# A Fourier gate whose norms and inner products are taken from the features in space

## The chip, the cores and the metric

The kernel runs on one core of one Trainium2 chip. The metric is the device time of one execution in microseconds; the median of 3 executions of the kernel before is 333.0 us (332.04 to 333.19). The core has these engines: PE (TensorE, matrix products; PEld is its weight load), DVE (VectorE), ACT (ScalarE, activation functions), POOL (GpSimd) and SP (which starts transfers). Each engine works through its own list of instructions in order and waits on semaphores for the others.

## The reference, cut to what matters

The program is a chain of seven layers in float32 on an input of 8 images, 32 channels, 16 x 16 points: group norm and deformable convolution, the Fourier gate, an attention with landmarks and a pseudo-inverse, a mixture of experts, four layers of linear attention, and a routed layer whose operations depend on the data. The change lies in the Fourier gate alone:

```
feat = gelu(batchnorm(conv2d(x, conv_w, padding=3, dilation=3)))     # 8 images, 16 channels
F2   = fft2(feat)                                                   # complex
qkv  = F2.reshape(B, 8, 2, N)                                       # heads of two channels; q = k = v
q    = qkv / sqrt(sum(re**2 + im**2, over N) + 1e-6)
attn = einsum('bhdn,bhen->bhde', q, conj(q)) * tau                  # 2 x 2 for each head, complex
attn = softmax(attn.real) + 1j * softmax(attn.imag)
out_f = abs(ifft2(attn @ qkv))
cg   = sigmoid(cg2_w * gelu(bn(conv1x1(F2.real, cg1_w))) + cg2_b)
gate = abs(ifft2(cg * F2))
y    = concatenate([out_f, gate]) + x
```

N is 256 points. For real a and b and their transforms A and B, the sum over N of A conj(B) is N times the sum over N of a b, which is real; so the norm of A is taken from a, and the imaginary part of the inner product is zero.

## The kernel before, in words

The 8 images x 16 channels of `feat` fill the 128 partitions, and the 256 points are the columns (tile `feat`, 128 x 256). The kernel is written by hand: each engine has one function (`_(pe)`, `_(act)`, `_(dve)` and so on), its order is the order of the text, and the semaphores tie them. `link` on DVE makes the next instruction wait for the end of this one. `then_inc(S["..."])` raises a semaphore, `wait_ge` waits for it. Small values of a partition stand in the columns of the tile `small`.

The gate goes as follows, and all of it stands between the convolution (L614) and the first layer norm of the tokens (L1329 by way of `centre`, L1476):

- ACT makes `feat` by a Gelu (L1119). PE transposes it (L621), ACT copies the transposed tile (L1121), and PE multiplies with a table of sines and cosines into `F2`, real and imaginary part side by side, 128 x 512 (L628). ACT copies that to SBUF (L1123).
- PE makes two products with a matrix that swaps the two channels of a head: of `feat` (L625, bank 5) and of `F2` (L633, bank 4). A float32 matmul shows in the trace as two instructions ("passes") or more; a transpose as one.
- The branch of the gate: PE L632, then on ACT a Gelu (L1126) and a Sigmoid (L1127) make `cg`; DVE multiplies `F2` by it (L1449, two halves, semaphore `gated`); PE transposes the result (L646), ACT copies it (L1131), PE transforms it back (L651), ACT squares (L1137), DVE adds real and imaginary squares (L1473), ACT takes the root (L1139, semaphore `abs` at 2).
- The branch of the attention: DVE takes sums of squares and products of `F2` and its swapped copy `mixed` (L1437 to L1445, a custom instruction that reads out a sum, so two records each), adds the 1e-6 (L1452, `l2_sum`), ACT takes roots (L1129), DVE works out the four scores of each head (L1454 to L1461, `sm2_in`), ACT takes their exponentials (L1133), DVE makes the weights and mixes `feat` and the swapped `feat` in space (L1463 to L1471), ACT takes the root (L1135, `abs` at 1).
- PE gathers both into the tokens (L659, first from `outf`, then from `gatef`), and its last product lets DVE go on with the layer norm (L1329). Between these steps PE runs `keep_busy(n)`: n products of 512 columns, two passes each, whose results nobody reads (L528). In this stretch there are `keep_busy(4)` ahead of the wait for `gated`, `keep_busy(4)` behind L651, and `keep_busy(7)` behind L659.

On ACT an `ACT_TABLE_LOAD` is put in by the compiler where a function needs another table than the one before it; the text of the kernel doesn't name it, and the trace gives it the line of the activation that it serves. The layers behind the gate wait for its output by semaphores, each in turn; the weights for them are all loaded before the gate begins (`late_in`), but for the records of the routed layer, whose transfers are started by SP when PE, at the end of the landmark attention, raises `oT_mm`, or by the steps of the routed layer themselves.

Of the kernel before, what the change touches and what calls it, by code (L numbers as in the profile page):

```python
# [20 lines left out]
ACT = mybir.ActivationFunctionType  # L21
# [3 lines left out]
N = HH * WW  # L25
# [79 lines left out]
FFT_EV = {"featT": 1, "f2": 2, "gT": 3}  # L105


class Own:
# [5 lines left out]
    def link(self, ins):  # L114
        self.n += 1
        ins.then_inc(self.sem, 1)
        self.eng.wait_ge(self.sem, self.n)
# [7 lines left out]
def build(nc, x, cst, w32, par, rows, toep, w_out, moe_w1, moe_w2, moe_b2, am, fm, codes, rec_a, rec_b, out):  # L125
    ctx = ExitStack()
    with ctx:
# [3 lines left out]
        S = {n: ctx.enter_context(nc.semaphore(n)) for n in SEMS}  # L131
        ps = [ctx.enter_context(nc.psum_tensor(f"ps{i}", [P, 512], F32))[:, :] for i in range(8)]
# [13 lines left out]
        def cst_(n):  # L146
            return cstb[:, CST[n][0]:CST[n][1]]
# [31 lines left out]
        small = sb("small", 512)  # L179
# [16 lines left out]
        feat = sb("feat", N)  # L196
        featT = sb("featT", PT * P).rearrange("p (t n) -> p t n", t=PT)
        F2 = ar(18432, 2 * N)
        mixed = ar(18944, 2 * N)
# [321 lines left out]
        def _(pe):  # L521
# [3 lines left out]
            def keep_busy(count, lhs=None, rhs=None, bank=7, cols=512):  # L525

                for _ in range(count):
                    mm(ps[bank][:, 0:cols], ident if lhs is None else lhs, (xC if rhs is None else rhs)[:, 0:cols],  # L528
                       start=True, stop=True)
# [103 lines left out]
            mm(ps[4], cst_("swap"), F2, start=True, stop=True).then_inc(S["swap_mm"], 1)  # L633
# [8 lines left out]
            keep_busy(4)  # L642
# [11 lines left out]
            keep_busy(4)  # L654
# [418 lines left out]
        def _(act):  # L1073
# [47 lines left out]
            af(featT.rearrange("p t n -> p (t n)"), ps[2][:, 0:PT * P], ACT.Copy).then_inc(S["fft_ev"], 1)  # L1121
            act.wait_ge(S["fft_mm"], FFT_MM["f2"])
# [5 lines left out]
            act.wait_ge(S["l2_sum"], 1)  # L1128
            af(small[:, 18:20], small[:, 16:18], ACT.Sqrt).then_inc(S["l2_std"], 1)  # L1129
            act.wait_ge(S["fft_mm"], FFT_MM["gT"])  # L1130
            af(gT.rearrange("p a t n -> p (a t n)"), ps[7], ACT.Copy).then_inc(S["fft_ev"], 1)  # L1131
            act.wait_ge(S["sm2_in"], 1)
            af(small[:, 28:32], small[:, 28:32], ACT.Exp).then_inc(S["sm2_exp"], 1)  # L1133
# [183 lines left out]
        def _(dve):  # L1317
# [110 lines left out]
            for reach in (1, 2, 4, 8, 16, 32):  # L1428
# [5 lines left out]
            Fp, fp = ps[4], ps[5][:, 0:N]  # L1434
            dve.wait_ge(S["fft_ev"], FFT_EV["f2"])
            sm = small
            link(v_.tensor_tensor_reduce(scr, F2, F2, 1.0, 0.0, ALU.mult, ALU.add, sm[:, 16:17]))  # L1437
            dve.wait_ge(S["swap_mm"], 2)
            link(v_.tensor_copy(mixed, Fp))
            link(v_.tensor_tensor_reduce(scr, mixed, mixed, 1.0, 0.0, ALU.mult, ALU.add, sm[:, 17:18]))  # L1440
            link(v_.tensor_copy(sm[:, 20:21], sm[:, 16:17]))
            link(v_.tensor_tensor_reduce(scr, F2, mixed, 1.0, 0.0, ALU.mult, ALU.add, sm[:, 21:22]))
            link(v_.tensor_tensor_reduce(scr[:, 0:N], F2[:, N:2 * N], mixed[:, 0:N], 1.0, 0.0, ALU.mult, ALU.add,
                                         sm[:, 22:23]))
            link(v_.tensor_tensor_reduce(scr[:, 0:N], F2[:, 0:N], mixed[:, N:2 * N], 1.0, 0.0, ALU.mult, ALU.add,  # L1445
                                         sm[:, 23:24]))
            dve.wait_ge(S["cg_act"], 1)
            for a in range(2):
                tt_(gated[:, a * N:a * N + N], F2[:, a * N:a * N + N], cg, ALU.mult).then_inc(S["gated"], 1)  # L1449
            link(tt_(sm[:, 23:24], sm[:, 22:23], sm[:, 23:24], ALU.subtract))  # L1450
            link(v_.memset(sm[:, 22:23], 0.0))
            ts_(sm[:, 16:18], sm[:, 16:18], 1e-6, None, ALU.add).then_inc(S["l2_sum"], 1)  # L1452
            dve.wait_ge(S["l2_std"], 1)
# [7 lines left out]
            tt_(ex, pairs, sm[:, 20:22].unsqueeze(2).to_broadcast([P, 2, 2]), ALU.subtract).then_inc(S["sm2_in"], 1)  # L1461
            dve.wait_ge(S["sm2_exp"], 1)
# [426 lines left out]
```

## Time and profile before

| | |
|---|---|
| median of 3 executions | 333.0 us (332.04 to 333.19) |
| the profiled execution's own time | 331.74 us |
| its span, first to last instruction | 330.0 us |
| granted TensorE clock, mean | 0.982 of full speed |
| busy: PE, PEld, DVE, ACT, POOL | 294.5, 199.4, 189.0, 154.4, 35.1 us |
| the Fourier gate, `feat` to the layer norm | 89.91 to 110.03 us |

Times in the rows are microseconds from the span's start. An engine's busy time counts its filling products too: PE's 89% is in part `keep_busy`. In a row, the share in brackets at the end is the idle time of the engine before it and what released it. Ends of matmuls are modelled, and neighbouring ones overlap in the record; the distance from start to start is the safer measure.

### The profile page before, as it was taken

Reading aid. Unit: us, or ns where it says so; the run is one execution under the profiler, and the core shown is the slowest. Engines: PE = TensorE matmul, PEld = TensorE weight load, DVE = VectorE, ACT = ScalarE, POOL = GpSimd, SP = SyncE. Lnnn points to the kernel's source line nnn. Section 1 sums busy time; section 2 is a strip of 40 time slices with the busy share of each in tenths; the row PEclk is TensorE's granted clock in tenths of the full one; section 3 lists DMA queues with packets and bytes.
Section 4 is the critical chain, followed back from the end, with each engine's and each line's share of the span. In section 5 each row is a group of like instructions: output and inputs, shape, how many; then the busy total and the mean of one; then the engine's idle time right before and its main releaser. Section 6 shows DMA issues by size and latency. Waiting matters only on the chain.

```text
span 330.0 us, 6721 instructions
## 1 busy us (share of the span) xinstructions
PE 294.5 (89%) x2064; PEld 199.4 (60%) x2064; DVE 189.0 (57%) x452; ACT 154.4 (47%) x336; POOL 35.1 (11%) x34
## 2 busy tenths in 40 slices
PE   7999999999999989999999989989996779777980
PEld 3665677777444437898999645668952266226620
DVE  4594998883346676478887564462261156225720
ACT  2097766667154256445566033112203448644840
POOL 5300062000100014000220000024200000000010
PEclk9999999999999999999999999999998799999997
DMA  2954300000000000000000033333100100000000
GB/s 84 248 113 89 88 9 2 2 0 2 2 0 0 0 1 2 0 2 0 3 0 0 0 58 62 68 68 63 31 2 3 21 2 0 19 19 0 0 18 32
DMA packets 9386, 9.17 MB, mean 28 GB/s; under 512 B 4080, under 2 KB 8944, under 8 KB 9072
## 3 DMA queue, kind: packets, MB, share of 16 engines
q1 hardware_dynamic: 9096, 8.53, 11.7%
q8 instruction: 15, 0.25, 0.3%
q10 hardware_dynamic: 264, 0.30, 0.3%
q14 instruction: 11, 0.08, 0.1%
HBM read 8.57 MB, written 0.26 MB: 27 GB/s over the span
## 4 chain that ended last, share of the span: by engine, by line
PE 32%; DVE 10%; issue 4%; ACT 2%; DMA 2%; DVEq 2%; SPq 0%; POOL 0%; ACTq 0%; POOLq 0%
PE ps L759 3%; PE ps L765 3%; DMA recA<-rec_a 2%; PE ps L915 2%; PE ps L999 2%; PE ps L1055 2%; PE ps L1002 2%; PE ps L528 2%; PE ps L1047 2%; PE ps L905 1%; PE ps L897 1%; PE ps L1012 1%; PE ps L776 1%; PE ps L806 1%; DVE arena L1562 1%
## 5 line engine op out<-in xcount | busy, mean ns | idle before, releaser
L528 PE MATMUL ps<-xC,cstb 128*128 128x512 f32 (+3 forms) x134 | 57.3, 554 | 0.0
L1407 DVE TENSOR_TENSOR arena<-arena 128x512 f32 x72 | 44.3, 684 | 7.8 <-ACT arena L1107 4.6
L1114 ACT ACTIVATE arena<-ps 128x512 f32<-128x512 f32 x72 | 37.7, 603 | 15.7 <-PE ps L585 15.6
L528 PEld LDWEIGHTS ps<-xC,cstb 128*128 128x128 f32 x134 | 23.7, 192 | 24.1 <-issue 23.9
L585 PE MATMUL ps<-cstb,arena 128*128 128x128 f32 x288 | 36.3, 277 | 0.7 <-DVE arena L1407 0.7
L585 PEld LDWEIGHTS ps<-cstb,arena 128*128 128x128 f32 x288 | 31.0, 140 | 9.4 <-DVE arena L1407 8.6
L593 PE MATMUL ps<-arena 128*32 128x256 f32 x288 | 19.2, 385 | 0.0
L1275 ACT ACTIVATE arena<-ps,rmax 128x256 f32<-128x256 f32 x32 | 14.7, 479 | 2.6 <-DVE rmax L1738 2.4
L759 PE MATMUL ps<-arena 128*128 128x160 f32 x96 | 14.5, 304 | 0.3 <-DVE arena L1590 0.3
L1055 PE MATMUL ps<-arena,w2c 128*32 128x512 f32 x32 | 12.0, 719 | 1.9 <-ACT arena L1306 1.9
L497 POOL TENSOR_TENSOR arena<-w32b,cstb 128x1024 f32<-128x1024 f32 x4 | 7.6, 1893 | 57.5 <-PEq L891 45.8
L759 PEld LDWEIGHTS ps<-arena 128*128 128x128 f32 x96 | 13.3, 190 | 0.5 <-DVE arena L1590 0.4
L1306 ACT ACTIVATE arena<-ps,w2c 128x512 f32<-128x512 f32 x16 | 9.7, 688 | 7.6 <-PE ps L1047 7.6
L999 PE MATMUL ps<-cstb 128*128 128x256 f32 x28 | 9.3, 414 | 3.3 <-ACT arena L1275 3.3
L1082 ACT ACTIVATE small<-small 128x16 f32<-128x16 f32 x5 | 1.1, 216 | 23.3 <-DVE small L1333 22.4
L1738 DVE TENSOR_REDUCE rmax<-ps 128x2 f32<-128x512 f32 x16 | 10.3, 683 | 2.8 <-PE ps L990 2.5
L765 PE MATMUL ps<-arena,bdY 128*128 128x64 f32 x96 | 11.5, 273 | 0.3 <-DVE arena L1581 0.3
L765 PEld LDWEIGHTS ps<-arena,bdY 128*128 128x128 f32 x96 | 11.2, 192 | 0.5 <-DVE arena L1581 0.5
L593 PEld LDWEIGHTS ps<-arena 128*32 128x32 f32 x288 | 7.5, 109 | 6.3 <-ACT arena L1114 3.1
L453 POOL TENSOR_SCALAR cgw<-cstb,parb 128x128 f32<-128x128 f32 x1 | 7.1, 7096 | 33.3 <-DMA codeB<-codes 33.3
L506 POOL TENSOR_TENSOR ln_a<-tC,hC 128x512 f32<-128x512 f32 x1 | 1.3, 1268 | 84.6 <-DVE hC L1792 84.6
L1002 PE MATMUL ps<-cstb,arena 128*128 128x128 f32 x64 | 9.3, 273 | 0.0
(373 smaller groups left out, 529.0 us busy)
## 6 DMA issues: line engine op xcount, KB each, us to landing
arena<-rec_a SPq DMA_DIRECT2D x19, 128.5 KB
toepb<-toep SPq DMA_DIRECT2D x1, 1536.0 KB
w32b<-w SPq DMA_DIRECT2D x1, 1225.0 KB
cstb<-cst SPq DMA_DIRECT2D x1, 1044.0 KB
recA<-rec_a SPq DMA_DIRECT2D x4, 128.5 KB
arena<-rec_b SPq DMA_DIRECT2D x19, 16.5 KB
w1b<-moe_w SPq DMA_DIRECT2D x1, 264.0 KB
xC<-x SPq DMA_DIRECT2D x1, 256.0 KB, 2.6
```

The costliest lines, as they stand in the source:

```text
L528: mm(ps[bank][:, 0:cols], ident if lhs is None else lhs, (xC if rhs is None else rhs)[:, 0:cols], start=True, stop=True)
L585: last = tr(ps[c % BI][:, (q * PT + t) * P:(q * PT + t + 1) * P], ST[:, c, t, q * 8:q * 8 + 8, :], ident)
L593: last = mm(ps[4 + g][32 * bi:32 * bi + 32, 0:N], GS[:, g, q, bi, k, :], SQ[:, g * BI + bi, q, :], start=False, stop=last_one and q == PT - 1,
L759: last = mm(ps[q][:, 160 * j:160 * j + 160], bdY[:, b, :], YV[:, b, :], start=True, stop=True)
L765: last = mm(ps[q][:, 320 + 64 * j:384 + 64 * j], bdY2[:, 2 * q + j, :, :], pG[:, 2 * q:2 * q + 2, :], start=True, stop=True)
L999: mm(ps[a][:, 0:N], ident, cstb[:, 0:N], start=True, stop=True)
L1002: last = tr(ps[a][:, (u * PT + t) * P:(u * PT + t + 1) * P], pr[:, a * 512 + t * N + u * P:a * 512 + t * N + u * P + P], ident)
L1055: last = mm(ps[1][32 * bi:32 * bi + 32, :], w2c[:, 0:C], f1[:, 512 * bi:512 * bi + 512], start=True, stop=True)
L1114: af(SQ[:, c].rearrange("p q n -> p (q n)"), ps[c % BI], ACT.Copy).then_inc(S["s_ev"], 1)
L1275: last = af(pr[:, b * 512 + t * N:b * 512 + t * N + N], ps[b][:, t * N:t * N + N], ACT.Exp, bias=rmax[:, 2 * b + t:2 * b + t + 1], accum_o ...
L1407: tt_(ST[:, c], hy.unsqueeze(3).to_broadcast([P, PT, 16, 16]), hx.unsqueeze(2).to_broadcast([P, PT, 16, 16]), ALU.mult).then_inc(S["prod"], 1)
L1738: v_.tensor_reduce(rmax[:, 2 * b:2 * b + 2], arr3(ps[b], N), AX.X, ALU.max, negate=True).then_inc(S["sc_max"], 1)
```

## The change

PE's product of the swap matrix with `F2` (two passes) is gone, and both `keep_busy(4)` around the inverse transform become `keep_busy(2)`. On DVE the sums are taken over `feat` and over its swapped copy (256 columns instead of 512), scaled by N; this begins when `feat` is there instead of `F2`; the two sums of the imaginary part are gone, and their columns are set to zero. The scores are worked out ahead of the wait for `cg_act`, and the two multiplications by `cg` stand behind them. On ACT the root of the norms stands ahead of the copy of `F2`, between the Gelu of `feat` and the Gelu of `cg`; the exponential of the scores stands behind the Sigmoid and ahead of the copy of `gT`.

```diff
--- before.py
+++ after.py
@@ -630,7 +630,6 @@
             pe.wait_ge(S["fft_ev"], FFT_EV["f2"])
             pe.wait_ge(S["pool_bd"], 5)
             mm(ps[6][:, 0:N], cgw, F2[:, 0:N], start=True, stop=True).then_inc(S["fft_mm"], 1)
-            mm(ps[4], cst_("swap"), F2, start=True, stop=True).then_inc(S["swap_mm"], 1)
 
             pe.wait_ge(S["x1_ready"], 2 * BG)
             mm(ps[1], zeros, cstb[:, 0:512], start=True, stop=False, skip_group_check=True)
@@ -639,7 +638,7 @@
                     mm(ps[1][:, (t * BG + g) * P:(t * BG + g + 1) * P],
                        x1C[:, g * N + t * P:g * N + t * P + P], ident, start=False, stop=False,
                        skip_group_check=True)
-            keep_busy(4)
+            keep_busy(2)
             pe.wait_ge(S["gated"], 2)
             for a in range(2):
                 for t in range(PT):
@@ -651,7 +650,7 @@
                 last = mm(ps[2], gT[:, a, t, :], dft[:, t, a * N:a * N + 2 * N], start=(n == 0), stop=(n == 3))
             last.then_inc(S["fft_mm"], 1)
 
-            keep_busy(4)
+            keep_busy(2)
             T1 = ps[1].rearrange("p (t b c) -> p t b c", t=PT, b=B)
             for n, src in enumerate((outf, gatef)):
                 pe.wait_ge(S["abs"], n + 1)
@@ -1119,18 +1118,18 @@
             af(feat, ps[0][:, 0:N], ACT.Gelu, bias=small[:, 13:14], scale=small[:, 12:13]).then_inc(S["feat"], 1)
             act.wait_ge(S["fft_mm"], FFT_MM["featT"])
             af(featT.rearrange("p t n -> p (t n)"), ps[2][:, 0:PT * P], ACT.Copy).then_inc(S["fft_ev"], 1)
+            act.wait_ge(S["l2_sum"], 1)
+            af(small[:, 18:20], small[:, 16:18], ACT.Sqrt).then_inc(S["l2_std"], 1)
             act.wait_ge(S["fft_mm"], FFT_MM["f2"])
             af(F2, ps[3], ACT.Copy).then_inc(S["fft_ev"], 1)
 
             act.wait_ge(S["fft_mm"], FFT_MM["cg"])
             own.link(af(cg, ps[6][:, 0:N], ACT.Gelu, bias=small[:, 15:16], scale=small[:, 14:15]))
             af(cg, cg, ACT.Sigmoid, bias=par_("cg2_b"), scale=par_("cg2_w")).then_inc(S["cg_act"], 1)
-            act.wait_ge(S["l2_sum"], 1)
-            af(small[:, 18:20], small[:, 16:18], ACT.Sqrt).then_inc(S["l2_std"], 1)
+            act.wait_ge(S["sm2_in"], 1)
+            af(small[:, 28:32], small[:, 28:32], ACT.Exp).then_inc(S["sm2_exp"], 1)
             act.wait_ge(S["fft_mm"], FFT_MM["gT"])
             af(gT.rearrange("p a t n -> p (a t n)"), ps[7], ACT.Copy).then_inc(S["fft_ev"], 1)
-            act.wait_ge(S["sm2_in"], 1)
-            af(small[:, 28:32], small[:, 28:32], ACT.Exp).then_inc(S["sm2_exp"], 1)
             act.wait_ge(S["sum_sq"], 1)
             af(outf, outf, ACT.Sqrt).then_inc(S["abs"], 1)
             act.wait_ge(S["fft_mm"], FFT_MM["inv"])
@@ -1431,25 +1430,23 @@
                          ALU.max))
             dve.sem_inc(S["code_set"], 1)
 
-            Fp, fp = ps[4], ps[5][:, 0:N]
-            dve.wait_ge(S["fft_ev"], FFT_EV["f2"])
+            fp = ps[5][:, 0:N]
+            pair = mixed[:, 0:N]
             sm = small
-            link(v_.tensor_tensor_reduce(scr, F2, F2, 1.0, 0.0, ALU.mult, ALU.add, sm[:, 16:17]))
-            dve.wait_ge(S["swap_mm"], 2)
-            link(v_.tensor_copy(mixed, Fp))
-            link(v_.tensor_tensor_reduce(scr, mixed, mixed, 1.0, 0.0, ALU.mult, ALU.add, sm[:, 17:18]))
+
+            def inner(a, b, at):
+
+                link(v_.tensor_tensor_reduce(scr[:, 0:N], a, b, float(N), 0.0, ALU.mult, ALU.add, sm[:, at:at + 1]))
+
+            dve.wait_ge(S["feat"], 1)
+            inner(feat, feat, 16)
             link(v_.tensor_copy(sm[:, 20:21], sm[:, 16:17]))
-            link(v_.tensor_tensor_reduce(scr, F2, mixed, 1.0, 0.0, ALU.mult, ALU.add, sm[:, 21:22]))
-            link(v_.tensor_tensor_reduce(scr[:, 0:N], F2[:, N:2 * N], mixed[:, 0:N], 1.0, 0.0, ALU.mult, ALU.add,
-                                         sm[:, 22:23]))
-            link(v_.tensor_tensor_reduce(scr[:, 0:N], F2[:, 0:N], mixed[:, N:2 * N], 1.0, 0.0, ALU.mult, ALU.add,
-                                         sm[:, 23:24]))
-            dve.wait_ge(S["cg_act"], 1)
-            for a in range(2):
-                tt_(gated[:, a * N:a * N + N], F2[:, a * N:a * N + N], cg, ALU.mult).then_inc(S["gated"], 1)
-            link(tt_(sm[:, 23:24], sm[:, 22:23], sm[:, 23:24], ALU.subtract))
-            link(v_.memset(sm[:, 22:23], 0.0))
+            dve.wait_ge(S["swap_mm"], 1)
+            link(v_.tensor_copy(pair, fp))
+            inner(pair, pair, 17)
             ts_(sm[:, 16:18], sm[:, 16:18], 1e-6, None, ALU.add).then_inc(S["l2_sum"], 1)
+            inner(feat, pair, 21)
+            link(v_.memset(sm[:, 22:24], 0.0))
             dve.wait_ge(S["l2_std"], 1)
             link(v_.reciprocal(sm[:, 18:20], sm[:, 18:20]))
 
@@ -1459,6 +1456,9 @@
             link(v_.tensor_reduce(sm[:, 20:22], pairs, AX.X, ALU.max))
             ex = sm[:, 28:32].rearrange("p (r s) -> p r s", r=2)
             tt_(ex, pairs, sm[:, 20:22].unsqueeze(2).to_broadcast([P, 2, 2]), ALU.subtract).then_inc(S["sm2_in"], 1)
+            dve.wait_ge(S["cg_act"], 1)
+            for a in range(2):
+                tt_(gated[:, a * N:a * N + N], F2[:, a * N:a * N + N], cg, ALU.mult).then_inc(S["gated"], 1)
             dve.wait_ge(S["sm2_exp"], 1)
             link(v_.tensor_reduce(sm[:, 20:22], ex, AX.X, ALU.add))
             link(v_.reciprocal(sm[:, 20:22], sm[:, 20:22]))
```

## Rows read from the trace of the kernel before

**Rows 1.** Timeline of PE, 84 to 113 us: start, length, engine, line, operation, shapes, count, idle.
```profile
90.52 0.44 PE L621 MATMUL ps<-cstb,feat 128*128 128x128 f32 x2 [0.67 <-ACT feat L1119]
...
91.43 1.98 PE L628 MATMUL ps<-cstb,featT 128*128 128x512 f32 x4
...
94.64 1.02 PE L633 MATMUL ps<-arena,cstb 128*128 128x512 f32 x2
...
97.25 3.60 PE L528 MATMUL ps<-xC,cstb 128*128 128x512 f32 x8
100.68 0.60 PE L646 MATMUL ps<-cstb,arena 128*128 128x128 f32 x4
101.97 3.70 PE L651 MATMUL ps<-cstb,arena 128*128 128x512 f32 x8 [0.69 <-ACT arena L1131]
...
108.94 0.61 PE L659 MATMUL ps<-cstb,outf 128*128 128x128 f32 x4
109.38 0.61 PE L659 MATMUL ps<-cstb,gatef 128*128 128x128 f32 x4
```

**Rows 2.** Timeline of ACT, 84 to 113 us.
```profile
91.00 0.38 ACT L1121 ACTIVATE featT<-ps 128x256 f32<-128x256 f32 x1 [0.53 <-PE ps L621]
93.45 0.60 ACT L1123 ACTIVATE arena<-ps 128x512 f32<-128x512 f32 x1 [2.08 <-PE ps L628]
94.84 0.56 ACT L1126 ACTIVATE cg<-ps,small 128x256 f32<-128x256 f32 x1 [0.79 <-PE ps L632]
95.42 1.28 ACT L1127 ACT_TABLE_LOAD   x1
96.72 0.60 ACT L1127 ACTIVATE cg<-cg,parb 128x256 f32<-128x256 f32 x1
97.33 1.28 ACT L1129 ACT_TABLE_LOAD   x1
100.28 0.20 ACT L1129 ACTIVATE small<-small 128x2 f32<-128x2 f32 x1 [1.66 <-DVE small L1452]
101.32 0.60 ACT L1131 ACTIVATE arena<-ps 128x512 f32<-128x512 f32 x1 [0.84 <-PE ps L646]
101.93 1.28 ACT L1133 ACT_TABLE_LOAD   x1
103.23 0.21 ACT L1133 ACTIVATE small<-small 128x4 f32<-128x4 f32 x1
...
107.64 0.58 ACT L1137 ACTIVATE arena<-ps 128x512 f32<-128x512 f32 x1
108.71 0.42 ACT L1139 ACTIVATE gatef<-gatef 128x256 f32<-128x256 f32 x1 [0.49 <-DVE gatef L1473]
```

**Rows 3.** Timeline of DVE, 84 to 113 us.
```profile
94.08 0.69 DVE L1437 CUSTOM_DVE_ANT_0 scr<-arena 128x512 f32<-128x512 f32 x1 [7.47 <-ACT arena L1123]
...
98.15 0.42 DVE L1443 CUSTOM_DVE_ANT_0 scr<-arena 128x256 f32<-128x256 f32 x1
...
99.08 0.76 DVE L1449 TENSOR_TENSOR arena<-arena,cg 128x256 f32<-128x256 f32 x2
...
103.46 0.16 DVE L1463 TENSOR_REDUCE small<-small 128x2 f32<-128x4 f32 x1 [1.88 <-ACT small L1133]
...
106.86 0.42 DVE L1471 TENSOR_TENSOR outf<-arena 128x256 f32<-128x256 f32 x1
...
110.03 0.69 DVE L1329 TENSOR_REDUCE small<-ps 128x16 f32<-128x512 f32 x1 [1.35 <-PE ps L659]
```

**Rows 4.** Windows of the routed layer: length, busy time and count by engine, PEclk, DMA.
```profile
252.00:256.00 4.00, 2.63 (x14) 0.86 (x14) 0.22 (x1) 1.21 (x3) 0.00 (x0) 0.69 0.02 4
...
288.00:292.00 4.00, 2.12 (x16) 0.82 (x16) 0.66 (x5) 1.07 (x2) 0.00 (x0) 1.00 0.06 18
```

**Rows 5.** Timeline of PE in the routed layer, two steps with the same product.
```profile
253.47 2.02 PE L1047 MATMUL ps<-hC,recA 32*128 32x512 f32 x5
...
289.80 1.10 PE L1047 MATMUL ps<-hC,recA 32*128 32x512 f32 x5
```

## The prediction

> **What bounds the kernel now.** I read the timelines of the three working engines over the gate's stretch first, because the change touches nothing else, and looked in each for the step that the last one, the layer norm's first reduction on DVE, waits for. That reduction starts at 110.03, 0.04 us after PE's last gathering product ends [rows 1, 3]. PE's own row is nearly gapless backwards from there: the gathering products start at 108.94; before them lie L651 (from 101.97, eight passes) and eight filler passes, together 16 passes in 6.97 us, 0.43 us each [rows 1]. L651 waited 0.69 us for ACT's copy of gT, and that copy for the four transposes of L646 [rows 1, 2].
>
> Why did L646 start at 100.68? The product `gated` was complete at 99.08 + 0.76 = 99.84 on DVE [rows 3], 0.84 us earlier. But the filler from 97.25 takes 3.43 us to the start of L646 [rows 1]: PE itself was the last to be ready. So DVE, whose inner products hold back the multiplication by `cg` (`cg` is ready at 96.72 + 0.60 = 97.32, the multiplication starts at 99.08) [rows 2, 3], and the filler are two bounds of nearly the same length, and the change takes from both. A shortened DVE chain alone would gain nothing here, and less filler alone at most those 0.84 us at this place.
>
> The attention branch is late too, but not last: `outf` is complete at 106.86 + 0.42 = 107.28 [rows 3], its root some 0.46 us later, and PE gathers it only at 108.94, when its filler is over [rows 1]. The gate branch ends at 108.71 + 0.42 = 109.13, and its products start at 109.38 [rows 1, 2], 0.25 us after. Both branches have to come forward if the second filler's cut is to count.
>
> **The change part by part.** Times are those of the profiled execution.
>
> *PE.* The swap of `F2` (two passes at 0.43) and two of the first four fillers (four passes at 0.43) go: 0.86 + 1.72 = 2.58 us less ahead of L646. PE would be ready at 100.68 - 2.58 = 98.10. Nothing reads the removed bank any more.
>
> *DVE, sums.* A sum over 256 columns takes 0.42 us (L1443), over 512 columns 0.69 (L1437) [rows 3], each plus about 0.05 for the read-out. The first now starts when `feat` is there, about 90.5 (DVE was idle for 7.47 us up to 94.08 [rows 3]), and ends at about 91.0. The swapped `feat` is complete before PE starts L628 at 91.43 [rows 1]. No row has a copy of 256 columns out of PSUM; I bound it by the 256- and the 512-column operations, 0.42 and 0.69, and take 0.48. Copy 91.5 to 92.0, sum to 92.5, the addition 0.2: `l2_sum` at about 92.7, at worst 92.9.
>
> *ACT, the root of the norms.* It stands now ahead of the copy of `F2`, so a late `l2_sum` would delay everything. The copy of featT ends at 91.38; a table load of 1.28 runs to 92.68, ahead of the wait (as the load of L1129 at 97.33 ran while its activation came at 100.28 [rows 2]), the root takes 0.20, and ACT is free at 92.9 (93.2 with the upper bound). `F2` is copied at 93.45 [rows 2], when PE releases it. The cover is 0.5 us, 0.25 at the bound: cost nothing.
>
> *ACT, the extra table.* Here the change pays. Before, the two Gelus had only copies between them: `cg`'s Gelu at 94.84 has no load ahead of it. Now the root's table is in, and a reload is needed. It will stand behind the copy of `F2`: L1133's load came at 101.93, directly behind the copy L1131, though ACT had been idle ahead of that copy [rows 2]. So: copy ends 94.05, load 94.07 to 95.35, Gelu 95.37 to 95.93, load 95.95 to 97.23, Sigmoid 97.25 to 97.85. The idle 0.79 us ahead of L1126 hides part of it; the net delay of `cg` is 0.53 us. Bounds: 0 if the load were placed earlier, 1.30 if it ran after the wait (then `cg` at 98.6). A row shows load and activation start to start as 1.30 us (95.42 to 96.72), with nothing more between [rows 2].
>
> The Trainium skill, page "ScalarE: Activation LUTs", section "What ACT_TABLE_LOAD costs", gives about 1283 ns for the load, which the rows repeat as 1.28, but adds a drain of about 1380 ns to each switch. By that the reload would cost 1.38 us more than I count, and the gain would be 2.27 instead of 3.65. The 0.02 us that the row leaves between load and Sigmoid speak against it here.
>
> *DVE, scores and the multiplication.* After the root (92.9) the scores need reciprocal, two scalings, a maximum and a subtraction, under 2 us in the trace, as they and a table load fit between 100.28 and 103.23 [rows 2]; done before 95, where DVE has nothing else. Then it waits for `cg_act`. This wait now stands ahead of the softmax, but the exponential stands behind the Sigmoid on ACT anyway. Multiplication: 97.88 to 98.64 (0.76 [rows 3]). That is later than PE's 98.10, so DVE, and by it ACT's chain of two loads, is the new bound here.
>
> *Transposes, copy, inverse transform.* After a wait two transposes take 0.44 us (L621) and each further one 0.11 (four in 0.44 from start to start at L659) [rows 1]: from 98.69 to 99.35. The copy gT stands behind the exponential now. If that needs a load after the Sigmoid, it runs 97.86 to 99.14 and the exponential (0.21 [rows 2]) ends at 99.36: just in time, the copy starts at 99.39. Copy to 99.99, L651 at 100.04 instead of 101.97: **1.93 us** earlier. This is less than PE's 2.58, because 0.65 us of the cut become a wait for `gated`.
>
> *The second filler.* Four passes fewer, 4 x 0.43 = **1.72 us**, if both branches are ready. L659 could start at 108.94 - 1.93 - 1.72 = 105.29, and the products of `gatef` at 105.73. `outf`: exponential 99.36, then the same DVE steps as from 103.46 to 107.28 (3.82 us [rows 3]), 103.2, root by 103.7. `gatef`: L651 would end at 100.04 + 3.70 = 103.74, and from the square's start to the root's end it is 109.13 - 107.64 = 1.49 us [rows 2]: 105.27; plus the 0.25 seen above 105.52, 0.2 us before it is needed. Both just fit.
>
> *Behind the gate.* All later work starts from PE's last gathering product, directly or in turn; the transfers of the records start by `oT_mm` or by the routed steps and move with it. I let it all shift.
>
> **Sum:** 1.93 + 1.72 = 3.65 us. Span 330.0 - 3.65 = 326.35, the profiled execution's 331.74 becomes 328.1. That execution lies 1.3 us below the median of 333.0, below the lowest of the three as well; taken from the median, the forecast is 333.0 - 3.65 = 329.35, told as 329.3.
>
> **The rivals.**
>
> *A. Part of the gain (330 to 331.3).* The arrangement is tight in three places: gT's copy behind the exponential (0.03 us of margin), `outf`'s root ahead of the square (0.1), `gatef` ahead of its products (0.2). Each delay beyond its margin counts one to one. For it: ACT now carries five loads in a row where it waited before. Against it: every duration has a row of its own. With the reload after the wait (bound above), `cg` is 0.77 later and the gain 2.9: 330.1. Without it A holds 12 in 100. The drain that the Trainium skill states ("ScalarE: Activation LUTs") would give 2.27 and 330.7; that rule has 3 in 100 of its own, A in all 15.
>
> *B. Slower, by TensorE's clock.* The fillers keep PE running, and the change takes eight passes and adds a gap of about 0.5 us ahead of L646, followed by 0.69 ahead of L651. If the granted clock falls there from 2.4 to 1.2 GHz, PE's chain stretches: the same product took 2.02 us in one step and 1.10 in another [rows 5], the first of them near a window whose mean clock was 0.69 [rows 4], so by a factor of 1.84. L651 (3.53), the filler (1.72) and the gathering (0.88) would take 5.1 us more: 333.0 - 3.65 + 5.1 = 334.5. It decides from about 8 us of low clock in PE-bound work (3.65 / 0.46). For it: such a fall exists in this kernel. Against it: the clock is at full through this stretch, and from 288 to 292 it stayed at 1.00 with PE busy for 2.12 of 4 us [rows 4], while I expect about 2.9 of 4 between 98 and 102. 5 in 100.
>
> *C. No change (332 to 334).* A low stretch of half that length, or one more in the routed layer by the changed position (1.10 to 2.02 on one product, and the like on its neighbours), cancels half or more of the gain. Also: the later layers follow something that does not move. I find no such thing; 8 in 100.
>
> *D. More than 4.1 us,* if the low stretch at 252 us disappears by the shift: 4 in 100.
>
> **How the numbers follow.** The forecast, a gain of 3.2 to 4.1 us, gets 68 in 100. Its own range is 328.4 to 330.2, by the spread of the executions before. With most of A, and D's near edge, 8 in 10 lie from 327.9 to 331.8. A difference of 0.5% (1.67 us) is what a measurement here can tell from none. Faster: 68 + 15 + 4 = 87, less 1 for A's weak end, 0.86; within 0.09; slower 0.05.
>
> **What would show it.** Right: a third Gelu-side load at about 94.07 and the Gelu at 95.4; `F2` still copied at 93.45; L1449's successor starting at 97.9; L651 at 100.0; the gathering at 105.3 and the reduction at 106.4. Wrong: the copy of `F2` later than 93.5 (the root holds it), a gap of over 0.1 us ahead of gT's copy with the exponential in it, a wait ahead of the gathering products, or a PEclk below 1.00 between 96 and 112.

## The result, and the profile after

The changed kernel takes 328.23 us (median of 4, 327.77 to 328.74) against 333.05 us before (median of 4, 332.04 to 333.19): ratio 0.9879, 95% interval 0.9846 to 0.9911. Two further measurements of the same kernel gave 0.9891 (0.9863 to 0.9918) and 0.9865 (0.9818 to 0.9911). The forecast, 3.65 us of 333.0, is a ratio of 0.9890. The two medians themselves lie 4.82 us apart, more than forecast, and 328.23 is 1.1 us below the forecast 329.3; the last part comes back to this. The profiled execution took 328.04 us with a span of 326.2 us, 3.8 us shorter than before.

The comparison that doesn't depend on the rest of the kernel is the gate's own stretch, from the start of the Gelu that makes `feat` to the start of the layer norm's first reduction. Before it is 110.03 - 89.91 = 20.12 us; after, 106.46 - 89.98 = 16.48 us: **3.64 us** less. In the two other traces of the changed kernel it is 16.47 both times. It is used below as "the stretch". `feat` comes 0.07 us later here, so rows of after are to be read 0.07 lower against the forecast.

PE after, to be held against [rows 1] (line numbers are one lower behind the removed line):

```profile
94.72 1.02 PE L635 MATMUL ps<-cstb,zeros 128*128 128x512 f32 x2
...
96.47 1.88 PE L528 MATMUL ps<-xC,cstb 128*128 128x512 f32 x4
98.77 0.66 PE L645 MATMUL ps<-cstb,arena 128*128 128x128 f32 x4 [0.42 <-DVE arena L1461]
100.11 3.70 PE L650 MATMUL ps<-cstb,arena 128*128 128x512 f32 x8 [0.69 <-ACT arena L1132]
103.65 1.88 PE L528 MATMUL ps<-xC,cstb 128*128 128x512 f32 x4
105.37 0.61 PE L658 MATMUL ps<-cstb,outf 128*128 128x128 f32 x4
105.81 0.61 PE L658 MATMUL ps<-cstb,gatef 128*128 128x128 f32 x4
```

The removed product lets L635 start at 94.72; the filler has four passes instead of eight; L645 waits 0.42 us for DVE (with the 0.07 taken off it starts at 98.70, 0.60 us behind the 98.10 at which PE was to be ready), L650 0.69 us for ACT as before. After L650 PE does not wait again: the gathering starts at 105.37, directly behind the second filler.

ACT after [rows 2]:

```profile
91.48 1.28 ACT L1122 ACT_TABLE_LOAD   x1
92.77 0.20 ACT L1122 ACTIVATE small<-small 128x2 f32<-128x2 f32 x1
93.53 0.60 ACT L1124 ACTIVATE arena<-ps 128x512 f32<-128x512 f32 x1 [0.56 <-PE ps L628]
94.15 1.28 ACT L1127 ACT_TABLE_LOAD   x1
95.45 0.56 ACT L1127 ACTIVATE cg<-ps,small 128x256 f32<-128x256 f32 x1
96.03 1.28 ACT L1128 ACT_TABLE_LOAD   x1
97.32 0.60 ACT L1128 ACTIVATE cg<-cg,parb 128x256 f32<-128x256 f32 x1
97.94 1.28 ACT L1130 ACT_TABLE_LOAD   x1
99.23 0.20 ACT L1130 ACTIVATE small<-small 128x4 f32<-128x4 f32 x1
99.46 0.60 ACT L1132 ACTIVATE arena<-ps 128x512 f32<-128x512 f32 x1
...
103.85 0.60 ACT L1136 ACTIVATE arena<-ps 128x512 f32<-128x512 f32 x1
104.94 0.42 ACT L1138 ACTIVATE gatef<-gatef 128x256 f32<-128x256 f32 x1 [0.49 <-DVE gatef L1473]
```

The extra load is the one at 94.15, of L1127, the Gelu of `cg`. Between 94.15 and 99.43 ACT is never idle by more than 0.03 us: three loads, each with its activation behind it. The copy of gT (L1132) starts 0.03 us after the exponential (L1130) ends; PE's transposes (L645, 98.77 + 0.66) end at the same 99.43, so these rows don't tell which of the two held it.

DVE after [rows 3]:

```profile
92.52 0.17 DVE L1447 TENSOR_SCALAR small<-small 128x2 f32<-128x2 f32 x1
...
94.09 0.17 DVE L1458 TENSOR_TENSOR small<-small 128x4 f32<-128x4 f32 x1
97.95 0.76 DVE L1461 TENSOR_TENSOR arena<-arena,cg 128x256 f32<-128x256 f32 x2 [3.70 <-ACT cg L1128]
...
106.46 0.69 DVE L1328 TENSOR_REDUCE small<-ps 128x16 f32<-128x512 f32 x1 [1.55 <-PE ps L658]
```

`l2_sum` is made at 92.52 to 92.69, the scores are complete at 94.26, and DVE then waits 3.70 us for `cg`.

### The profile page after: what moved, and what is told of

The parts are those of the page before. It is cut to its first block, busy times and chain, and to the rows that moved or that the text cites. A ratio compares the mean times of both kernels' runs of the same rounds, so it can differ in the third digit from the quotient of the medians.

```text
span 326.2 us, 6697 instructions
## 1 busy us (share of the span) xinstructions
PE 291.2 (89%) x2054; PEld 198.1 (61%) x2054; DVE 186.8 (57%) x447; ACT 155.9 (48%) x337; POOL 37.9 (12%) x34
## 4 chain that ended last, share of the span: by engine, by line
PE 32%; DVE 10%; issue 4%; ACT 2%; DMA 2%; DVEq 2%; SPq 0%; POOL 0%; ACTq 0%; POOLq 0%
PE ps L758 4%; PE ps L764 3%; DMA recA<-rec_a 2%; PE ps L914 2%; PE ps L998 2%; PE ps L1001 2%; PE ps L1054 2%; PE ps L528 2%; PE ps L904 1%; PE ps L1046 1%; PE ps L896 1%; PE ps L1011 1%; PE ps L775 1%; PE ps L805 1%; DVE arena L1562 1%
## 5 line engine op out<-in xcount | busy, mean ns | idle before, releaser
L528 PE MATMUL ps<-xC,cstb 128*128 128x512 f32 (+3 forms) x126 | 54.8, 559 | 0.0
L528 PEld LDWEIGHTS ps<-xC,cstb 128*128 128x128 f32 x126 | 22.6, 195 | 22.6 <-issue 22.3
L453 POOL TENSOR_SCALAR cgw<-cstb,parb 128x128 f32<-128x128 f32 x1 | 9.8, 9842 | 30.5 <-DMA codeB<-codes 30.5
```

## The experiments

Each is compared with executions of the kernel before taken beside it. "Stretch" is from its one trace, as defined above; in brackets is the difference from before's 20.12.

| kernel | ratio to before (95%) | stretch, us |
|---|---|---|
| changed kernel, again | 0.9891 (0.9863 to 0.9918) | 16.47 (-3.65) |
| changed kernel, third | 0.9865 (0.9818 to 0.9911) | 16.47 (-3.65) |
| fillers only | 0.9975 (0.9959 to 0.9992) | 19.30 (-0.82) |
| all but the fillers | 0.9987 (0.9962 to 1.0011) | 19.27 (-0.85) |
| order and fillers, sums as before | 1.0020 (0.9989 to 1.0051) | 20.39 (+0.27) |
| multiplication first | 0.9925 (0.9897 to 0.9954) | 16.91 (-3.21) |
| ACT's order of before | 0.9913 (0.9883 to 0.9942) | 17.64 (-2.48) |
| no fillers | 0.9937 (0.9912 to 0.9962) | 19.14 (-0.98) |
| Newton root | 0.9879 (0.9850 to 0.9908) | 15.96 (-4.16) |
| Newton root, shorter filler | 0.9867 (0.9834 to 0.9900) | 15.65 (-4.47) |
| the same, again | 0.9864 (0.9816 to 0.9911) | 15.65 (-4.47) |

### Fillers only

```diff
-            keep_busy(4)
+            keep_busy(2)
             pe.wait_ge(S["gated"], 2)
...
-            keep_busy(4)
+            keep_busy(2)
             T1 = ps[1].rearrange(...)
```

> The kernel before with both four-product fillers around the inverse transform cut to two, nothing else. My theory: DVE's inner products hold the multiplication by cg, so the transposes move only from 100.68 to about 99.95 (the multiplication is complete at 99.84), and the second cut is lost because the attention branch, whose chain moves by the same 0.73 us, becomes the last. Gain about 0.75 us, of the 3.65. Rival: filler was the bound and the rest is decoration: six or eight passes of 0.43 us, gain 2.5 to 3.5 us.

PE in that kernel (its `feat` came at 90.69, 0.78 us later than before's):

```profile
100.69 0.66 PE L646 MATMUL ps<-cstb,arena 128*128 128x128 f32 x4 [0.78 <-DVE arena L1449]
...
107.85 0.71 PE L659 MATMUL ps<-cstb,outf 128*128 128x128 f32 x4 [0.40 <-ACT outf L1135]
109.24 0.71 PE L659 MATMUL ps<-cstb,gatef 128*128 128x128 f32 x4 [0.68 <-ACT gatef L1139]
```

L646 comes 0.77 us earlier relative to `feat`, then PE waits twice at the gathering (0.40 and 0.68 us) for the roots of the two branches. The stretch is 0.82 us shorter: my theory, and its forecast of 0.75, hold. Eight passes are 3.44 us of PE time, and three quarters of that did not shorten the stretch: waits stand in their place. The 0.68 us ends with the gate branch: its root, behind the square that had stood behind `outf`'s root, ended at 109.19.

### All but the fillers

```diff
 (the changed kernel with)
-            keep_busy(2)
+            keep_busy(4)
             pe.wait_ge(S["gated"], 2)
...
-            keep_busy(2)
+            keep_busy(4)
             T1 = ps[1].rearrange(...)
```

> The changed kernel with both fillers back at four products. My theory: PE loses only the two passes of the removed product ahead of the transposes, 0.86 us, and everything behind it shifts by that: gain against before 0.86 us (transposes at 99.8, gathering at 108.1). Rival: the shorter chain on DVE is what counts and PE's fillers were slack: gain over 2 us.

PE in that kernel (`feat` at 90.05):

```profile
99.97 0.60 PE L645 MATMUL ps<-cstb,arena 128*128 128x128 f32 x4
101.26 3.70 PE L650 MATMUL ps<-cstb,arena 128*128 128x512 f32 x8 [0.69 <-ACT arena L1132]
...
108.23 0.61 PE L658 MATMUL ps<-cstb,outf 128*128 128x128 f32 x4
```

No wait ahead of L645 and none ahead of the gathering: PE is the bound throughout, and the gain is the removed product's two passes, 0.85 us in the stretch. The timed ratio can't tell this from no change. So neither part is the cause of the gain by itself: 0.82 and 0.85 apart, 3.64 together. The earlier scores and the shorter chain on DVE gave nothing here beyond the two passes.

### Order and fillers, sums as before

```diff
 (the kernel before with both fillers at two, and)
+            dve.wait_ge(S["cg_act"], 1)
+            for a in range(2):
+                tt_(gated[:, a * N:a * N + N], F2[:, a * N:a * N + N], cg, ALU.mult).then_inc(S["gated"], 1)
             link(v_.tensor_tensor_reduce(scr[:, 0:N], F2[:, N:2 * N], mixed[:, 0:N], ...
             link(v_.tensor_tensor_reduce(scr[:, 0:N], F2[:, 0:N], mixed[:, N:2 * N], ...
-            dve.wait_ge(S["cg_act"], 1)
-            for a in range(2):
-                tt_(gated[...
 (ACT)
-            act.wait_ge(S["l2_sum"], 1)
-            af(small[:, 18:20], small[:, 16:18], ACT.Sqrt).then_inc(S["l2_std"], 1)
             act.wait_ge(S["fft_mm"], FFT_MM["gT"])
             af(gT.rearrange("p a t n -> p (a t n)"), ps[7], ACT.Copy).then_inc(S["fft_ev"], 1)
+            act.wait_ge(S["l2_sum"], 1)
+            af(small[:, 18:20], small[:, 16:18], ACT.Sqrt).then_inc(S["l2_std"], 1)
```

> The kernel before with its sums over the transforms kept, but the multiplication by cg moved ahead of the last two sums on DVE, the copy of gT ahead of the root on ACT, and both fillers cut to two. It asks whether the order alone gives the gain. My theory: the gate branch comes forward by about 0.9 us (multiplication at 98.2 instead of 99.1), but the attention branch is as long as before, outf at 107.3, and its root, and the square behind it, are now the last: gain at most 0.2 us. Rival: the inner products in space are not what counts, the order and the fillers are: gain 1.5 us or more.

PE in that kernel, and the clock there in windows of 2 us (`feat` at 90.15). A window's row has its length, the busy time and count of PE, PEld, DVE, ACT and POOL, then the granted clock as a share of full speed, and two figures on transfers:

```profile
100.56 3.70 PE L651 MATMUL ps<-cstb,arena 128*128 128x512 f32 x8 [0.69 <-ACT arena L1129]
...
107.89 0.91 PE L659 MATMUL ps<-cstb,outf 128*128 128x128 f32 x4 [1.91 <-ACT outf L1135]
109.28 1.22 PE L659 MATMUL ps<-cstb,gatef 128*128 128x128 f32 x4 [0.49 <-ACT gatef L1139]
```

```profile
106.00:108.00 2.00, 0.11 (x1) 0.12 (x2) 1.32 (x3) 0.58 (x2) 0.00 (x0) 1.00 0.00 0
108.00:110.00 2.00, 1.51 (x7) 1.22 (x8) 0.42 (x1) 0.73 (x2) 0.00 (x0) 0.57 0.00 0
```

The gate branch comes forward as expected (the inverse transform starts at 100.56, relative to `feat` 1.65 us earlier than before), but the attention branch hardly does (`outf` is complete 0.14 us earlier), and PE stands idle for 1.91 us ahead of the gathering. I expected a gain of up to 0.2 us and got a loss of 0.27: behind that idle time the granted clock is at 0.57 from 108 to 110, and the eight gathering products, 0.61 us for each four before, take 0.91 and 1.22. From the start of the last four to the reduction it is 1.26 us, against 0.75 in the kernel with the fillers alone, where the clock stayed at 1.00; without these 0.51 us the stretch would be 0.24 us shorter than before (an estimate), so the branches did what was expected and the clock is what I had not counted. The rival, that order and fillers do it without the shorter sums, falls for this order, which leaves the root of the norms behind the copy of gT; no other order with the long sums was run.

### Multiplication first

```diff
 (the changed kernel with)
+            dve.wait_ge(S["cg_act"], 1)
+            for a in range(2):
+                tt_(gated[:, a * N:a * N + N], F2[:, a * N:a * N + N], cg, ALU.mult).then_inc(S["gated"], 1)
             dve.wait_ge(S["l2_std"], 1)
             link(v_.reciprocal(sm[:, 18:20], sm[:, 18:20]))
...
-            dve.wait_ge(S["cg_act"], 1)
-            for a in range(2):
-                tt_(gated[...
             dve.wait_ge(S["sm2_exp"], 1)
```

> The changed kernel with the multiplication by cg put back ahead of the scores on DVE; ACT's order stays. My theory: the scores then start at 98.7 instead of 93.2, the exponential ends at about 100.1 and the copy of gT, which stands behind it on ACT, comes at 100.1 instead of 99.46; 0.65 us slower than the changed kernel, a gain against before of 3.0. Rival: the scores are off the path and it makes no difference (3.65); that would mean that the exponential does not hold the copy.

ACT in that kernel (`feat` at 90.72, 0.74 us later than in the changed kernel):

```profile
98.67 1.28 ACT L1130 ACT_TABLE_LOAD   x1
100.54 0.21 ACT L1130 ACTIVATE small<-small 128x4 f32<-128x4 f32 x1 [0.59 <-DVE small L1461]
100.65 0.58 ACT L1132 ACTIVATE arena<-ps 128x512 f32<-128x512 f32 x1
```

The exponential waits 0.59 us for the scores and the copy of gT waits for it, as said, so the rival falls. The size is 0.43 us, not 0.65: the exponential comes 0.57 us later than in the changed kernel relative to `feat`, and the copy starts 0.11 us behind the exponential's start, overlapping its end. I had it start only after the end. In the changed kernel the copy stood 0.23 us behind the exponential's start, so by this the exponential had 0.12 us of room there, and it was the end of the transposes that released the copy. In the kernel before and in the one with all but the fillers, where no exponential stands in the way, the copy starts 0.04 us behind the transposes' end; in the changed kernel it is 0.03.

### ACT's order of before

```diff
 (the kernel above with)
-            act.wait_ge(S["l2_sum"], 1)
-            af(small[:, 18:20], small[:, 16:18], ACT.Sqrt).then_inc(S["l2_std"], 1)
             act.wait_ge(S["fft_mm"], FFT_MM["f2"])
...
             af(cg, cg, ACT.Sigmoid, bias=par_("cg2_b"), scale=par_("cg2_w")).then_inc(S["cg_act"], 1)
-            act.wait_ge(S["sm2_in"], 1)
-            af(small[:, 28:32], small[:, 28:32], ACT.Exp).then_inc(S["sm2_exp"], 1)
+            act.wait_ge(S["l2_sum"], 1)
+            af(small[:, 18:20], small[:, 16:18], ACT.Sqrt).then_inc(S["l2_std"], 1)
             act.wait_ge(S["fft_mm"], FFT_MM["gT"])
             af(gT.rearrange("p a t n -> p (a t n)"), ps[7], ACT.Copy).then_inc(S["fft_ev"], 1)
+            act.wait_ge(S["sm2_in"], 1)
+            af(small[:, 28:32], small[:, 28:32], ACT.Exp).then_inc(S["sm2_exp"], 1)
```

> The changed kernel with ACT's order of before (root of the norms behind the Sigmoid, exponential behind the copy of gT) and the multiplication by cg ahead of the scores. No extra table load ahead of cg's Gelu. My theory: cg is ready 0.53 us earlier, L650 starts at about 99.6 instead of 100.1, but the exponential comes only at 100.9, outf's chain ends 1.6 us later and the square waits behind outf's root, so gatef is gathered at about 107.0 instead of 105.8: 1.2 us slower than the changed kernel, gain against before 2.4. Rival: the extra load is the more expensive of the two, then this order is as fast as the changed kernel or faster by 0.5.

PE in that kernel (`feat` at 89.98, as in the changed one):

```profile
99.65 3.70 PE L650 MATMUL ps<-cstb,arena 128*128 128x512 f32 x8 [0.69 <-ACT arena L1130]
...
105.47 0.71 PE L658 MATMUL ps<-cstb,outf 128*128 128x128 f32 x4 [0.40 <-ACT outf L1134]
106.87 0.71 PE L658 MATMUL ps<-cstb,gatef 128*128 128x128 f32 x4 [0.68 <-ACT gatef L1138]
```

L650 starts 0.46 us earlier, and PE then waits 0.40 us for `outf` and 0.68 us for `gatef`. The stretch is 1.16 us longer than the changed kernel's (forecast 1.2). Two orders differ from the changed kernel, DVE's and ACT's; against the kernel with the multiplication first, which has the same order on DVE, ACT's order alone is 0.73 us. The extra table load is worth its price: it buys a root that is done before the Sigmoid, and with it the attention branch.

This run prices the reload as well. Its `feat` starts at 89.98, as in the changed kernel, and the Gelu of `cg`, with no load ahead of it, at 94.92 instead of 95.45, 0.53 us earlier:

```profile
94.92 0.56 ACT L1125 ACTIVATE cg<-ps,small 128x256 f32<-128x256 f32 x1 [0.79 <-PE ps L632]
```

### No fillers

```diff
 (the changed kernel with)
-            keep_busy(2)
             pe.wait_ge(S["gated"], 2)
...
-            keep_busy(2)
             T1 = ps[1].rearrange(...)
```

> The changed kernel with both fillers around the inverse transform taken out, PE idle there: about 2.3 us ahead of the transposes. Theory 1: the fillers keep the granted clock; without them it falls to half ahead of L650, whose eight passes take up to twice 3.5 us: 2 to 4 us slower than the changed kernel. Theory 2: the gap is too small a share to matter; PEclk stays at 1.00 and gatef's branch, complete at 105.4, becomes the last: 0.2 us faster.

PE and the clock in windows of 2 us:

```profile
98.93 0.75 PE L644 MATMUL ps<-cstb,arena 128*128 128x128 f32 x4 [2.14 <-DVE arena L1459]
100.36 6.58 PE L649 MATMUL ps<-cstb,arena 128*128 128x512 f32 x8 [0.69 <-ACT arena L1130]
```

```profile
96.00:98.00 2.00, 0.79 (x8) 0.60 (x6) 0.00 (x0) 1.97 (x3) 0.00 (x0) 1.00 0.00 0
98.00:100.00 2.00, 0.75 (x4) 0.42 (x4) 1.08 (x4) 1.85 (x4) 0.00 (x0) 0.84 0.00 0
100.00:102.00 2.00, 1.64 (x2) 0.84 (x3) 1.84 (x5) 1.59 (x2) 0.00 (x0) 0.50 0.00 0
```

After 2.14 us of idle PE the granted clock falls to 0.50, the lower level (1.2 GHz), while the transposes of L644 run: in finer windows it is 1.00 up to 99.3 and 0.50 from 99.5, ahead of the further 0.69 us of waiting. The eight passes of the inverse transform take 6.58 us instead of 3.70. The stretch is 2.66 us longer than the changed kernel's: theory 1. This is the mechanism of the prediction's rival B; its factor was put at 1.84, here it is 6.58 / 3.70 = 1.78. The trace shows one execution of twelve. Seven, the traced one among them, took 330.87 to 331.62 us at a mean clock of 0.966 to 0.970; four took 328.43 to 329.31 us at 0.980 or 0.981, within the changed kernel's own spread (327.70 to 329.89). So the fall may not come in each execution; no trace of the four is there to show it.

### Newton root

```diff
 (the changed kernel with)
-            act.wait_ge(S["l2_sum"], 1)
-            af(small[:, 18:20], small[:, 16:18], ACT.Sqrt).then_inc(S["l2_std"], 1)
...
-            ts_(sm[:, 16:18], sm[:, 16:18], 1e-6, None, ALU.add).then_inc(S["l2_sum"], 1)
+            link(ts_(sm[:, 16:18], sm[:, 16:18], 1e-6, None, ALU.add))
...
-            dve.wait_ge(S["l2_std"], 1)
-            link(v_.reciprocal(sm[:, 18:20], sm[:, 18:20]))
+            link(ts_(sm[:, 18:20].bitcast(I32), sm[:, 16:18].bitcast(I32), -0.5, float(0x5F3759DF), ALU.mult, ALU.add))
+            for _ in range(3):
+                link(tt_(sm[:, 24:26], sm[:, 18:20], sm[:, 18:20], ALU.mult))
+                link(stt(sm[:, 24:26], sm[:, 24:26], -0.5, sm[:, 16:18], ALU.mult, ALU.mult))
+                link(stt(sm[:, 18:20], sm[:, 24:26], 1.5, sm[:, 18:20], ALU.add, ALU.mult))
```

> The changed kernel with the root of the norms taken off ACT: DVE computes the reciprocal root from the bits and three Newton steps (ten small instructions of about 0.2 us), so ACT needs no root table between the two Gelus. This prices the reload. Theory: cg's Gelu starts at 94.9 instead of 95.45, the multiplication at 97.43, L650 at 99.6 instead of 100.1 and the gathering 0.5 us earlier; DVE's scores are complete by 96.3, ahead of the multiplication. 0.5 us faster than the changed kernel. Rival, a drain of 1.38 us with each table switch: 1.9 us faster or so, as far as PE's filler allows; rival, DVE's ten instructions run past 97.4 and hold the multiplication: no gain.

ACT, then DVE, in that kernel (`feat` at 90.22):

```profile
95.16 0.56 ACT L1125 ACTIVATE cg<-ps,small 128x256 f32<-128x256 f32 x1 [0.79 <-PE ps L632]
95.75 1.28 ACT L1126 ACT_TABLE_LOAD   x1
97.04 0.60 ACT L1126 ACTIVATE cg<-cg,parb 128x256 f32<-128x256 f32 x1
...
99.18 0.60 ACT L1130 ACTIVATE arena<-ps 128x512 f32<-128x512 f32 x1
```

```profile
96.23 0.16 DVE L1459 TENSOR_TENSOR small<-small 128x4 f32<-128x4 f32 x1
97.67 0.76 DVE L1462 TENSOR_TENSOR arena<-arena,cg 128x256 f32<-128x256 f32 x2 [1.28 <-ACT cg L1126]
```

No load stands ahead of L1125, the Gelu of `cg`. The scores are ready at 96.39 and the multiplication starts at 97.67, as soon as `cg` is there. The stretch is 0.52 us shorter than the changed kernel's, which is what the reload costs on the path after its cover: 1.30 - 0.79 = 0.51. By itself this does not rule out a drain on top of the load, since PE could hardly have given more back. Its filler, four passes at 0.43 us, ends as the multiplication does, at 98.43:

```profile
96.71 1.88 PE L528 MATMUL ps<-xC,cstb 128*128 128x512 f32 x4
98.49 0.66 PE L645 MATMUL ps<-cstb,arena 128*128 128x128 f32 x4
```

What rules it out is on ACT: in the changed kernel the copy of `F2` ends at 94.13, the load runs from 94.15 to 95.43 and the Gelu starts at 95.45; and the Gelu without the load, above, comes 0.53 us earlier, not 1.9.

### Newton root with a shorter second filler

```diff
 (the kernel above with)
-            keep_busy(2)
+            keep_busy(1)
             T1 = ps[1].rearrange(...)
```

> As the Newton kernel, with the second filler cut to one product. Theory: PE then waits for gatef's branch, complete at about 104.85; 0.2 us faster than the Newton kernel, 0.7 faster than the changed one. Rival: with PE less busy the clock falls, slower by over 1 us.

> The Newton kernel with the second filler at one product, again. Its gate stretch was 15.65 us against 16.48 of the changed kernel: 0.8 us faster in the stretch, and 0.8 us faster in time if the low clock stretches of the later layers fall as in the changed kernel; if cutting fillers further costs clock there, the time shows less than the stretch.

The stretch is 15.65 us both times, 0.31 us less than with the longer filler (0.2 expected) and 0.83 less than the changed kernel's. PE waits 0.29 us for `gatef` and starts 0.05 us after its root ends. The clock stays at 1.00 there, so the rival falls. In time it is 0.9867 and 0.9864, against 0.9891 and 0.9865 for the changed kernel beside it: faster than the kernel before without doubt, but that it beats the changed kernel is shown in the stretch alone; the intervals of the times overlap.

### The changed kernel again

> The changed kernel once more, beside the three below. Theory: 3.6 to 4.1 us faster than before; the gate's stretch as in its first trace to 0.1 us, while the stretches of low TensorE clock in the later layers lie elsewhere and move the span by up to 1 us. Rival: the low stretches are where they were, so the 0.3 us beyond the forecast in the median belong to the change.

> The changed kernel a third time, for its ratio beside the next one: 3.65 us faster than before, within 0.5; the gate's stretch from feat to the first reduction 16.5 us; the low stretches of the clock in the later layers as they fall.

Windows of 2 us in the first trace of the changed kernel, in the mixture of experts:

```profile
206.00:208.00 2.00, 2.00 (x10) 1.56 (x10) 0.42 (x1) 0.00 (x0) 0.00 (x0) 0.87 0.32 75
208.00:210.00 2.00, 2.00 (x5) 1.23 (x4) 0.99 (x2) 0.00 (x0) 0.00 (x0) 0.50 0.32 46
```

and in its third:

```profile
206.00:208.00 2.00, 2.00 (x11) 1.59 (x11) 0.42 (x1) 0.00 (x0) 0.00 (x0) 1.00 0.37 69
208.00:210.00 2.00, 2.00 (x7) 1.02 (x6) 1.63 (x3) 0.00 (x0) 0.00 (x0) 1.00 0.36 52
```

The same program had the low clock in the mixture of experts once and not in the two others; the product behind it (L885) started 107.63 us after the gate's end in the first, 106.23 in the second and 106.21 in the third, 1.4 us apart, of which a later wait took back all but 0.64. All three also have a low stretch in the routed layer, up to 256; it begins between 248 and 250 in the second, between 250 and 252 in the two others. That the low stretches of one and the same program lie differently is shown. How much each moves the span is not: the first trace, with one more of them, has the shortest span, 326.2 us against 326.8 and 326.3.

## Why the prediction was right

- **Which bound stands where.** The claim that DVE's sums and PE's filler were two bounds of nearly the same length was the point on which the forecast hung, and it was argued from rows before any run. Each alone was worth 0.82 and 0.85 us; the prediction said "at most 0.84" for the filler and nothing for the DVE chain alone; the 0.85 is the removed product's PE time. Both together gave 3.64.
- **The terms.** 1.93 us at L651: measured 1.86 + 0.07 = 1.93. 1.72 us for the second filler: the gathering comes 3.57 + 0.07 = 3.64 earlier, so 1.71. The reload's 0.53: the Gelu at 95.45 - 0.07 = 95.38 against the 95.37 forecast. DVE at 97.88, as forecast; L650 at 100.04, as forecast.
- **The cover of the root.** It ended at 92.97 and the copy of `F2` began at 93.53: 0.56 us of idle time on ACT against my 0.5, so the root did cost nothing. The unseen copy of 256 columns took 0.42 us, the lower bound.
- **Where it was off.** The 0.25 us that I read as the way from `gatef`'s root to its products is no such thing. In the kernel with the fillers alone the products start at 109.24 and the root had ended at 108.77 + 0.42 = 109.19, so 0.05 us. In [rows 1, 2] the distance was the four `outf` passes still running. The margin of that branch was 0.4, not 0.2. The margin ahead of gT's copy was likewise larger, 0.12 instead of 0.03, since the copy can start before the exponential ends. Both errors were to the careful side and changed no term.
- **The time itself.** 329.3 was forecast, 328.23 measured: 0.2 us below the forecast's own range of 328.4 to 330.2, inside the wider 327.9 to 331.8. The medians differ by 4.82 us where 3.65 was forecast, and by 4.13 and 4.43 in the two repeats. The gain in the stretch came out to 0.01 us, and what lies behind it shifted as a whole: from the gate's end to the last instruction it is 219.97 us before, and 219.74, 220.4 and 219.82 in the three traces of the changed kernel. Part of the rest is the base: it was the median of three executions, 333.0, and 331.94, 332.69 and 332.76 in later sets of 16 to 23. Part is the clock in whole executions. In the two repeats and what was taken beside them, the executions with the highest mean clock (0.985 or 0.986) have medians of 331.37 before (seven) and 327.80 after (three), 3.57 us apart; those at 0.980 to 0.982 have 332.70 (twenty) and 328.56 (four), 4.1 apart. Why the changed kernel seems to lose less at the lower mean clock is not shown, and the numbers of executions are small.
- **The rivals.** The slower one, by the clock, was real as a mechanism: two experiments met it, with 2.14 and 1.91 us of idle PE. The 0.42 us that the change adds did not, and the clock stays at 1.00 in the changed kernel's stretch. The drain of "ScalarE: Activation LUTs" in the Trainium skill ("What ACT_TABLE_LOAD costs", about 1380 ns with each switch) does not show in these chains: the first four loads of the changed kernel each stand 0.01 to 0.02 us from the activations before and behind them, and the reload delays the Gelu of `cg` by 0.53 us, not by 1.9. That page's table rule in the Trainium skill, to group activations by set ("Table sets: the hidden batching unit"), would speak against the changed order, which has five loads in the stretch where ACT's order of before has four. The runs show that here the order with more loads is 0.73 us faster on ACT's side alone, and 1.16 us together with DVE's order that goes with it, because the load costs about 0.52 us on one branch and unlocks the other. Doing without the root's table altogether gives the shortest stretch of the three.

## What to carry to other kernels

Where two engines' bounds end within a microsecond of each other, cut both or little moves; work out for each part what it gives alone, and expect both together to give more than the sum of the parts (3.64 against 0.82 + 0.85 here). Taking a sum from an earlier tensor helps twice, by its start and by its size: the sum of the norms ended 7.62 us earlier relative to `feat`, 3.57 by the start of DVE's first sum and 4.05 by the fewer and shorter steps from there, among which the multiplication by `cg` no longer stands. No run separates the two in the time, and either counts only if the small steps behind can be placed in idle time of the other engines. When a chain is shortened, shorten the filler with it, but leave enough that TensorE doesn't come to idle gaps like the two here, 1.9 and 2.1 us, behind which its clock was halved.

## What the runs showed of the hardware that was not expected

Two activations in a row can overlap on ACT: a copy started 0.11 us after an exponential that takes 0.21 us. The trace of before has the same between the root of `outf` and the square, which starts at 107.64 [rows 2]:

```profile
107.32 0.42 ACT L1135 ACTIVATE outf<-outf 128x256 f32<-128x256 f32 x1 [2.59 <-DVE outf L1471]
```

In two traces the granted clock fell to half just after PE had taken up its work again: behind 1.91 us of idle time, under the gathering products, and behind 2.14 us, under the transposes, from where it lasted through the inverse transform. In the kernel with the fillers alone, idle times of 0.78 and 0.69 us in a row, and later 0.40 and 0.68, left it at full, and so did 0.49 and 1.05 us with the multiplication first.

DVE reads the bits of a float as an integer, scales them and writes them back as an integer in one instruction of 0.17 us:

```profile
93.55 0.17 DVE L1448 TENSOR_SCALAR small<-small 128x2 int32<-128x2 int32 x1
```

With it a reciprocal root takes ten small steps, 1.97 us in all. They are longer than the table load of 1.28 us that they save, but they run while DVE would wait for `cg`, and so cost the path nothing.
